# Moving a rounding step from ScalarE to GpSimd, and 256 columns of a sum from VectorE to ScalarE, in a four-layer convolution kernel

## Chip, cores and metric

The kernel runs on one core of a Trainium2 chip, as one launch. The metric is device time in microseconds: the median over several executions of the same program. All times below are in microseconds unless they are marked ns. Engine names: PE is TensorE, DVE is VectorE, ACT is ScalarE, POOL is GpSimd, SP is SyncE, which here only issues DMAs.

## What is computed

The state `x` has shape 32x32x32x32 (batch, then three axes that each layer reads in its own way). Four layers follow one another, and each adds its result to the state:

```
x = x + L0(gn(x))   # locally connected 3x3, signs of the weights, batch norm, relu, sign * mean
x = x + L1(gn(x))   # locally connected 3x3, plain f32 weights
x = x + L2(gn(x))   # like L0, other weights
x = x + L3(gn(x))   # products of all pairs of a row's elements, then a matmul
```

`gn` is a group normalisation. In L0 and L2 the weights (9.4 million numbers, used once each) enter as `sign(w) * mean(|w|)`, so the kernel needs both the sign of every weight and the sum of the absolute values of all of them:

```
def binarize(x):
    scale = jnp.mean(jnp.abs(x))
    return jnp.sign(x) * scale
...
wb = binarize(weight)[0]
out = jnp.einsum('bchwk,ochwk->bohw', patches, wb)
```

## The kernel before

**Tiling.** The image has 8 blocks (`BLOCKS`) of four rows by 4 pieces (`PIECES`) of eight columns, so each of the first three layers is 32 chunks, numbered n = 4m + j. A chunk of weights is one DMA of 128 x 2304 f32 numbers (1152 KB) into a ring of 8 slots, `wring`. A piece of the state is 128 x 256 numbers. Pieces are normalised in an order of their own, numbered e: `order(m, j)` takes blocks 0 and 1 alternately for the first `FRONT` = 8 pieces and is 4m + j after that. A chunk needs its own piece and the pieces above and below it. `needed(n)` is the last of these, e = n + 4 for n from 4 to 27.

**What a chunk of the first and third layers takes.**

- SP issues the load of chunk n once both `signs_made` and `abs_made` say that chunk n - 8 has been read (line 284), since its slot is then free.
- DVE sums the absolute values of the first `ABS_DVE` = 2048 columns (line 738). After chunks with n % 4 = 3 and n % 4 = 0 it evacuates one half row of results from PSUM: a transpose (line 730) and a sum (line 732). It waits for the convolution there.
- ACT sums the absolute values of the other 256 columns (line 509, an `ACTIVATE` with a read of the accumulator behind it) and writes the signs of all 2304 columns in f16 (line 510). After n % 4 = 1 and 2 it squares a half row of results, 512 columns, also with an accumulator (line 537).
- The normalised pieces are f32 and are split in two f16 halves: the high half is the f32 value rounded to f16, the low half is the rest. For e < 8 DVE normalises, for e >= 8 POOL does, with a subtraction and a multiplication (line 265). In both cases **ACT makes the high half** (line 517, `high_half`) and **POOL the low half** (line 372, `low_half`), which reads the high half.
- POOL copies the chunk's own piece, both halves, to `near` (line 383). ACT's queue issues two DMAs of 32 KB which bring the rows above and below to `beyond` (line 526), once the piece `needed(n)` has been normalised.
- PE waits for `near`, `beyond` and the signs, then runs the chunk's matmuls (line 890).

**The order of each queue is written out by hand.** Iteration n of ACT is: high halves up to e = needed(n) + 2, the wait that conv n - 4 is done, the wait for piece needed(n) and the two `beyond` DMAs, the wait for sign n - 1, absolute sum n, sign n, and in some iterations the square. Iteration n of POOL is: for each new e up to needed(n) + 2 the two normalising instructions and the low half of piece e - 1; then `near` n. In both, iteration 3 takes e = 8 and 9, iteration 4 takes e = 10, and from there on each takes one, up to e = 31 in iteration 25. Iterations 26 to 31 normalise nothing. Absolute sums and signs 0 and 1 are put ahead of the loop, while the group normalisation's statistics are still being made.

`xn_ring` holds 4 normalised pieces in f32, and a piece may be written when the low half of the piece 4 before it has been made. An instruction of POOL that reads what the POOL instruction before it wrote waits on a semaphore for it, as ACT and DVE do too.

Of the kernel before, what the change touches and what calls it, by code (L numbers as in the profile page):

```python
# [23 lines left out]
CHUNKS = BLOCKS * PIECES  # L24
# [1 line left out]
REACH = TAPS * C  # L26
CHUNK = KINDS * COLS * REACH
PIECE = COLS * B
ABS_DVE = 2048
SLOTS = 8  # L30
FIRST_SLOT = (0, 0, 4)
FRONT = 8
PE_SUMS = (((0, 3), (3, 6)), ((0, 4), (4, 8)))
DVE_SQUARES = 5
XSLOTS = 4
# [38 lines left out]
def build(nc, x, w_conv, bias, gamma_beta, w_pairs, mats, sel_rows, sel_index, out):  # L74
    ctx = ExitStack()
    with ctx:
        def sb(name, shape, dt):
            return ctx.enter_context(nc.sbuf_tensor(name, shape, dt))

        def sem(name):  # L80
            return ctx.enter_context(nc.semaphore(name))

        def sems(name, n):
            return [sem(f"{name}{i}") for i in range(n)]
# [8 lines left out]
        xn_ring = sb("xn_ring", [P, XSLOTS, PIECE], F32)  # L93
# [17 lines left out]
        row_id = sb("row_id", [P, 1], F32)  # L111
        unused = sb("unused", [P, CHUNK - ABS_DVE], BF16)

# [39 lines left out]
        centred = sem("centred")  # L153
        xn_made = sem("xn_made")
        hi_made = sem("hi_made")
        front_made = sem("front_made")
        norm_made = sems("norm_made", 3)
        squares = sems("squares", 4)
# [52 lines left out]
        def blk(t, m):  # L211
            return t[:, m * BLOCK:(m + 1) * BLOCK]
# [4 lines left out]
        def normed(layer, m, j):  # L217
            aux = states[layer][1]
            first = (m + 1) * BLOCK + j * PIECE
            return aux[:, first:first + PIECE]  # L220

        def at(e):

            return (e % 2, e // 2) if e < FRONT else divmod(e, PIECES)
# [4 lines left out]
        def needed(n):  # L229

            m, j = divmod(n, PIECES)
            return order(min(m + 1, BLOCKS - 1), j)

        def slot(layer, n):
            return (n + FIRST_SLOT[layer]) % (PIECES if layer == 1 else SLOTS)
# [31 lines left out]
        def halves(layer, e):  # L267
            m, j = at(e)
            return normed(layer, m, j).bitcast(F16).rearrange("p (k n) -> p k n", k=2)
# [82 lines left out]
        def _(pool):  # L352
# [6 lines left out]
            def xn_of(layer, e, made):  # L359

                if layer != 1:
                    pool.wait_ge(norm_made[layer], e - XSLOTS + 1)
                sub, mul = normalise(pool, layer, e)
                sub().then_inc(centred, 1)
                centre[0] += 1
                pool.wait_ge(centred, centre[0])
                mul().then_inc(made, 1)

            def low_half(layer, e):
                pool.wait_ge(hi_made, CHUNKS * (layer // 2) + e + 1)  # L370
                hv = halves(layer, e)
                pool.tensor_tensor(hv[:, 1, :], xn_ring[:, e % XSLOTS, :], hv[:, 0, :], ALU.subtract).then_inc(norm_made[layer], 1)

# [13 lines left out]
            def sum_squares(layer, m):  # L387

                pool.wait_ge(squares[layer], m + 1)
                sq = blk(states[layer][1], m)  # L390
                width = BLOCK // 2
                while width > B:
                    pool.tensor_tensor(sq[:, 0:width], sq[:, 0:width], sq[:, width:2 * width], ALU.add).then_inc(halved, 1)  # L393
                    halvings[0] += 1
                    pool.wait_ge(halved, halvings[0])
                    width //= 2
                pool.tensor_tensor(red[:, 1, m * B:(m + 1) * B], sq[:, 0:B], sq[:, B:2 * B], ALU.add).then_inc(gn_red_pool[layer], 1)

            for layer in range(3):
                if layer < 2:  # L400
                    for m in range(DVE_SQUARES, BLOCKS):
                        sum_squares(layer, m)
                pool.wait_ge(gn_ready[layer], 1)
                ready = 0
                for n in range(CHUNKS):
                    upto = min(CHUNKS, needed(n) + 3)
                    for e in range(ready, upto):
                        if e >= FRONT:
                            xn_of(layer, e, norm_made[1] if layer == 1 else xn_made)
                        if layer != 1 and e:  # L410
                            low_half(layer, e - 1)
                        if layer != 1 and e == CHUNKS - 1:
                            low_half(layer, e)
                    ready = max(ready, upto)
                    copy_near(layer, n)
# [73 lines left out]
        def _(act):  # L489
# [13 lines left out]
            def sign_of(layer, n):  # L503
# [3 lines left out]
                if done:  # L507
                    act.wait_ge(signs_made, done)
                act.activation(unused[:, :], wring[:, slot(layer, n), ABS_DVE:], ACT.Abs, accum_out=abs_sums[:, CHUNKS + n:CHUNKS + n + 1])
                act.activation(signs[:, n % PIECES, :], wring[:, slot(layer, n), :], ACT.Sign).then_inc(signs_made, 1)  # L510

            def high_half(layer, e):
                if e < FRONT:
                    act.wait_ge(front_made, FRONT * layer + e + 1)
                else:
                    act.wait_ge(xn_made, (CHUNKS - FRONT) * (layer // 2) + e - FRONT + 1)
                act.activation(halves(layer, e)[:, 0, :], xn_ring[:, e % XSLOTS, :], ACT.Copy).then_inc(hi_made, 1)

            def load_beyond(layer, n):
# [28 lines left out]
            for layer in range(3):  # L548
                scratch = states[layer][1]
                if layer < 2:  # L550
                    square(layer)
                if layer == 0:
                    act.wait_ge(sums_cleared, 1)
                    act.wait_ge(sel_made, 1)
                if layer == 2:
                    act.wait_ge(conv_done, CHUNKS * 2)
                    act.wait_ge(row_summed, 2 * BLOCKS)
                if layer != 1:
                    for n in range(2):
                        sign_of(layer, n)  # L560
                width = MB if layer < 2 else 512
                take_root(rstd[:, 0:width], tmp_a[:, 0:width], (1, 3, 4)[layer])
                if layer == 1:
                    for n in range(CHUNKS):
                        m, j = divmod(n, PIECES)
                        used(1, n)
                        load_beyond(1, n)
                        act.activation(rest[:, j, :].rearrange("p (q h b) -> p q h b", q=2, b=B),  # L568
                                       state_a[:, 0:STATE].rearrange("p (q h b) -> p q h b", q=BLOCKS, b=B)
                                       [:, 2 * j:2 * j + 2, PIECES * m:PIECES * (m + 1), :], ACT.Copy).then_inc(rest_made, 1)  # L570
                        if n > PIECES and j in (1, 2):
                            square_row(2 * (m - 1) + j - 1)
                    for e in range(2 * BLOCKS - 2, 2 * BLOCKS):
                        square_row(e)
                    continue
                m2 = layer // 2
                ready = 0
                for n in range(CHUNKS):
                    upto = min(CHUNKS, needed(n) + 3)
                    for e in range(ready, upto):  # L580
                        high_half(layer, e)
                    ready = max(ready, upto)
                    used(layer, n)
                    load_beyond(layer, n)
                    if n >= 2:
                        sign_of(layer, n)
                    if n > PIECES and n % PIECES in (1, 2):
                        square_half(layer, 2 * (n // PIECES - 1) + n % PIECES - 1)
                for e in range(2 * BLOCKS - 2, 2 * BLOCKS):
                    square_half(layer, e)  # L590
                take_root(sc[:, 11:12], sc[:, 15:16], (2, 0, 5)[layer])

                for m in range(BLOCKS):
                    act.wait_ge(bn_affine[m2], m + 1)
                    act.activation(blk(scratch, m), blk(scratch, m), ACT.Relu,
                                   accum_out=relu_sums[:, m:m + 1]).then_inc(relu_made[m2], 1)
                for m in range(MASKS, BLOCKS):
                    act.wait_ge(relu_made[m2], m + 1)
                    act.activation(blk(scratch, m), blk(scratch, m), ACT.Sign).then_inc(masks_made[m2], 1)
# [43 lines left out]
        def _(dve):  # L643
# [30 lines left out]
            for layer in range(3):  # L674
# [59 lines left out]
                for n in range(CHUNKS):  # L734
                    dve.wait_ge(w_in[slot(layer, n)], 16 * loads(layer, n))
                    if n == 0 and m2:
                        dve.wait_ge(abs_red[0], 1)
                    dve.tensor_reduce(abs_sums[:, n:n + 1], wring[:, slot(layer, n), 0:ABS_DVE],  # L738
                                      X, ALU.add, apply_absolute_value=True).then_inc(abs_made, 1)
# [361 lines left out]
```

## Time and profile before

| | |
|---|---|
| median of 3 runs | 745.15 us (741.66 to 745.32) |
| the profiled execution | 743.5 us, of which the span from first to last instruction is 741.7 us |
| mean granted TensorE clock | 0.876 of full speed |
| busy share of the span | PE 69%, DVE 75%, ACT 59%, POOL 57% |
| first layer's chunk loop | about 45 to 140 us of the span |
| second layer's | about 190 to 312 us |
| third layer's | about 339 to 434 us |
| fourth layer | the rest |

The busy shares are averages over four layers whose limits differ; what the change is worth must be read from the chunk loops of the first and the third layer alone. A row of a timeline gives the start, the length, the engine, the line, the operation, output <- inputs and, in brackets, how long the engine had been idle and what released it. ACTq and SPq are the queues on which ACT and SP issue DMAs, so a row of ACTq is an issue and not a transfer. Lengths overlap the next instruction a little, so what an instruction costs its engine is the distance from its start to the next one's.

### The profile page before, as it was taken

The page shows a single profiled execution, that of the slowest core. Times are in us where ns is not written, and L with a number is a line of the kernel's source. Part 1 is how long each engine was busy: PE and PEld are TensorE (multiplying, and loading weights), DVE is VectorE, ACT ScalarE, POOL GpSimd, SP SyncE. Part 2 cuts the span into 40 slices and gives each one's busy share as a digit, 9 for nine tenths or more (in the row PEclk, how much of TensorE's full clock was granted, in tenths as well). Part 3 has the DMA queues.
Part 4 walks back from the last instruction along what each step waited for, and adds up shares of the span by engine and source line. Part 5 has one row for each costly group of instructions (what it writes and reads, how often), then busy time and mean ns, then how long its engine had stood idle before and what let it go on. Part 6 is the DMA issues. An engine that isn't in the chain of part 4 may idle for free.

```text
span 741.7 us, 53863 instructions
## 1 busy us (share of the span) xinstructions
PE 508.3 (69%) x24648; PEld 394.2 (53%) x24648; DVE 558.1 (75%) x691; ACT 436.2 (59%) x741; POOL 421.9 (57%) x653
## 2 busy tenths in 40 slices
PE   4548655418699999715756523726898898987997
PEld 4537655317578888604646521203565565554665
DVE  4798999898634323379999989954588787786887
ACT  5459999492112212136999938323567766675665
POOL 3389884004545541019888200546779878878662
PEclk9856899759799999975898975967899999999999
DMA  8949999400289999915999930015799999999995
GB/s 335 423 162 395 390 397 396 183 0 1 92 319 355 381 397 398 415 53 196 396 396 400 378 134 1 0 28 160 266 305 393 383 331 400 363 335 371 325 396 224
DMA packets 38882, 209.09 MB, mean 282 GB/s; under 512 B 7216, under 2 KB 14384, under 8 KB 18352
## 3 DMA queue, kind: packets, MB, share of 16 engines
q1 hardware_dynamic: 29376, 201.67, 71.5%
q10 hardware_dynamic: 9216, 6.30, 2.8%
q0 software_dynamic: 240, 0.53, 0.2%
q8 instruction: 22, 0.36, 0.2%
q14 instruction: 28, 0.23, 0.1%
HBM read 193.79 MB, written 4.19 MB: 267 GB/s over the span
## 4 chain that ended last, share of the span: by engine, by line
PE 34%; DVE 18%; DMA 17%; POOL 10%; issue 10%; ACT 8%; ACTq 2%; SPq 0%; POOLq 0%; DVEq 0%
PE psum L890 13%; DMA wring<-in_pairs 6%; PE psum L1003 6%; PE psum L977 5%; PE psum L914 5%; ACT signs L510 4%; DMA beyond<-state_a 3%; POOL xn_ring L265 3%; DMA wring<-in_w 3%; DMA beyond<-state_b 3%; DVE xn_ring L265 2%; PE psum L900 2%; DVE state_a L798 2%; ACTq L526 2%; ACT state_b L638 2%
## 5 line engine op out<-in xcount | busy, mean ns | idle before, releaser
L853 DVE TENSOR_TENSOR state_b<-psum,state_b 128x512 f32<-128x512 f32 x256 | 167.5, 686 | 56.9 <-ACT state_b L638 52.9
L890 PE MATMUL psum<-signs,near 64*32 64x96 f16 (+3 forms) x6528 | 125.0, 217 | 100.8 <-DMA beyond<-nothing 39.3
L638 ACT ACTIVATE state_b<-psum 128x512 f32<-128x512 f32 x256 | 142.0, 595 | 85.3 <-PE psum L977 79.4
L890 PEld LDWEIGHTS psum<-signs,near 64*32 64x32 f16 (+1 forms) x6528 | 112.3, 103 | 109.6 <-issue 109.2
L738 DVE TENSOR_REDUCE abs_sums<-wring 128x1 f32<-128x2048 f32 x64 | 142.9, 2276 | 0.1
L510 ACT ACTIVATE signs<-wring 128x2304 f16<-128x2304 f32 x64 | 135.0, 2109 | 0.0
L1003 PE MATMUL psum<-state_b,wring 128*32 128x32 f32 x8192 | 106.1, 202 | 10.9 <-issue 6.0
L1003 PEld LDWEIGHTS psum<-state_b,wring 128*32 128x32 f32 x8192 | 88.4, 114 | 42.0 <-issue 21.9
L977 PE MATMUL psum<-signs,sel 64*128 64x512 f16 x516 | 89.3, 400 | 25.3 <-POOL signs L428 13.9
L890 PE MATMUL psum<-wring,near 64*32 64x96 f32 (+5 forms) x3264 | 96.1, 240 | 15.3 <-DMA beyond<-nothing 10.7
L428 POOL COPY signs<-wring 64x512 f16<-64x512 f16 x130 | 85.8, 660 | 34.2 <-PE psum L977 27.7
L890 PEld LDWEIGHTS psum<-wring,near 64*32 64x32 f32 (+1 forms) x3264 | 86.6, 108 | 22.2 <-issue 22.2
L383 POOL COPY near<-state_b 128x512 f16<-128x512 f16 (+1 forms) x64 | 33.2, 521 | 72.5 <-PE psum L900 53.4
L709 DVE STREAM_TRANSPOSE state_b<-psum 128x512 f32<-128x512 f32 x16 | 11.5, 717 | 75.2 <-PE psum L900 75.2
L890 PE MATMUL psum<-signs,beyond 32*32 32x96 f16 (+2 forms) x2176 | 64.3, 215 | 0.0
L890 PEld LDWEIGHTS psum<-signs,beyond 32*32 32x32 f16 x2176 | 55.0, 101 | 4.7
L447 POOL COPY wring<-state_b 32x256 f32<-32x256 f32 x128 | 50.4, 394 | 10.1
L890 PE MATMUL psum<-wring,beyond 32*32 32x96 f32 (+2 forms) x1088 | 49.4, 239 | 1.3 <-issue 1.3
L977 PEld LDWEIGHTS psum<-signs,sel 64*128 64x128 f16 x516 | 23.6, 94 | 46.7 <-ACT state_b L638 24.8
L568 ACT ACTIVATE signs<-state_a 128x256 f32<-128x256 f32 x32 | 13.3, 417 | 59.2 <-issue 49.3
L393 POOL TENSOR_TENSOR state_b<-state_b 128x512 f32<-128x512 f32 (+3 forms) x24 | 16.7, 696 | 53.6 <-ACT state_b L501 52.2
L890 PEld LDWEIGHTS psum<-wring,beyond 32*32 32x32 f32 x1088 | 43.3, 106 | 5.2 <-issue 2.0
(151 smaller groups left out, 873.9 us busy)
## 6 DMA issues: line engine op xcount, KB each, us to landing
wring<-in_w SPq DMA_DIRECT2D x96, 1152.0 KB, 10.0
wring<-in_pairs SPq DMA_DIRECT2D x64, 1152.0 KB, 9.1
state_a<-in_x SPq DMA_DIRECT2D x8, 512.0 KB, 9.5
beyond<-state_b ACTq DMA_DIRECT2D x112, 32.0 KB, 5.9
wring<-signs SPq DMA_DIRECT2D x56, 64.0 KB, 4.9
out<-state_a SPq DMA_DIRECT2D x7, 512.0 KB, 11.3
beyond<-state_a ACTq DMA_DIRECT2D x56, 32.0 KB, 6.0
beyond<-nothing ACTq DMA_DIRECT2D x24, 32.0 KB, 4.2
```

Of the source, the lines that this page charges most:

```text
L265: return (lambda: eng.tensor_tensor(new, old, m_op, ALU.subtract)), (lambda: eng.tensor_tensor(new, new, r_op, ALU.mult))
L383: pool.tensor_copy(dst, src).then_inc(near_made, 1)
L428: pool.tensor_copy(ring[side * 2 * W:(side + 1) * 2 * W, k % GROUP, :].rearrange("p (g n) -> p g n", g=G), parts[0:2 * W, k // KPART % 2, ...
L447: pool.tensor_copy(own_x[beside * W:(beside + 1) * W, g % 2, cols], x_sq[g * W:(g + 1) * W, half, :]).then_inc(own_copied, 1)
L510: act.activation(signs[:, n % PIECES, :], wring[:, slot(layer, n), :], ACT.Sign).then_inc(signs_made, 1)
L638: act.activation(left[:, n % LSLOTS, :], psum[:, n % ASLOTS, :], ACT.Copy, scale=1.0 / HALF_SCALE / HALF_SCALE).then_inc(left_made, 1)
L738: dve.tensor_reduce(abs_sums[:, n:n + 1], wring[:, slot(layer, n), 0:ABS_DVE], X, ALU.add, apply_absolute_value=True).then_inc(abs_made, 1)
L853: dve.tensor_tensor(feats[:, n % FSLOTS, :], psum[:, ASLOTS + n % BSLOTS, :], left[:, n % LSLOTS, :], ALU.mult).then_inc(feats_made, 1)
L890: last = pe.matmul(psum[g * B:(g + 1) * B, bank, (a * C) % 512:(a * C) % 512 + (b - a) * C], acts[q, j, s, k, :], weights[q, j, kind, s, ( ...
L914: pe.matmul(psum[:, 4, first * B:end * B], same_half, by_h[:, h, first:end, :], start=(first == 0 and h == 0), stop=(h == H - 1), skip_gro ...
L977: last = pe.matmul(psum[:, bank, :], sel[half, t % PT * P:(t % PT + 1) * P], ring[half, t // PT, :], start=True, stop=True)
L1003: last = pe.matmul(psum[g * W:(g + 1) * W, 6 + s // HALF, col:col + B], wt[:, t % PT, c, g, :], f[:, g, c, :], start=False, stop=(t % (HAL ...
```

## The change

For e >= 8, in the first and third layers, the high half is made by POOL with a copy from f32 to f16 instead of by ACT. POOL then makes both halves of piece e right after normalising it, and waits for its own multiplication ahead of the high half and for its own high half ahead of the low half. The low halves of pieces 0 to 7 stay on POOL and their high halves on ACT, in the order in which they were (the low half of piece e - 1 behind the normalisation of e). `ABS_DVE` goes from 2048 to 1792: in every chunk of these two layers DVE sums 256 columns fewer and ACT 512 instead of 256. The scratch tile `unused` grows with it. Nothing else is changed.

```
-ABS_DVE = 2048
+ABS_DVE = 1792
...
+            def high_half(layer, e):                        # POOL
+                pool.wait_ge(xn_made, (CHUNKS - FRONT) * (layer // 2) + e - FRONT + 1)
+                pool.tensor_copy(halves(layer, e)[:, 0, :], xn_ring[:, e % XSLOTS, :]).then_inc(hi_pool, 1)
+                pool.wait_ge(hi_pool, (CHUNKS - FRONT) * (layer // 2) + e - FRONT + 1)
+
             def low_half(layer, e):
-                pool.wait_ge(hi_made, CHUNKS * (layer // 2) + e + 1)
+                if e < FRONT:
+                    pool.wait_ge(hi_made, FRONT * (layer // 2) + e + 1)
...
                         if e >= FRONT:
                             xn_of(layer, e, norm_made[1] if layer == 1 else xn_made)
-                        if layer != 1 and e:
+                        if layer != 1 and 0 < e <= FRONT:
                             low_half(layer, e - 1)
-                        if layer != 1 and e == CHUNKS - 1:
+                        if layer != 1 and e >= FRONT:
+                            high_half(layer, e)
                             low_half(layer, e)
...
             def high_half(layer, e):                        # ACT
-                if e < FRONT:
-                    act.wait_ge(front_made, FRONT * layer + e + 1)
-                else:
-                    act.wait_ge(xn_made, (CHUNKS - FRONT) * (layer // 2) + e - FRONT + 1)
+                act.wait_ge(front_made, FRONT * layer + e + 1)
...
                     upto = min(CHUNKS, needed(n) + 3)
-                    for e in range(ready, upto):
+                    for e in range(ready, min(upto, FRONT)):
                         high_half(layer, e)
```

## Rows read from the trace of the kernel before

**Rows 1.** Window, first layer: length, busy PE, PEld, DVE, ACT, POOL, clock, DMA share, GB/s
```profile
70.00:80.00 10.00, 5.49 (x465) 5.02 (x469) 9.96 (x7) 10.00 (x18) 8.48 (x13) 1.00 1.03 393
```

**Rows 2.** Timeline of ACT, one chunk of the first layer, next one's start
```profile
74.26 0.41 ACT L517 ACTIVATE state_b<-xn_ring 128x256 f16<-128x256 f32 x1
74.57 0.41 ACT L509 ACTIVATE unused<-wring 128x256 bf16<-128x256 f32 x1
...
74.97 2.11 ACT L510 ACTIVATE signs<-wring 128x2304 f16<-128x2304 f32 x1
76.98 0.41 ACT L517 ACTIVATE state_b<-xn_ring 128x256 f16<-128x256 f32 x1
```

**Rows 3.** Chain that ended last, first layer's end: start, length, what
```profile
131.35 6.31 DMA beyond<-state_b
...
137.75 1.63 PE psum L890 x128
```

**Rows 4.** Timeline of POOL, first layer, one iteration without idle time
```profile
52.86 0.73 POOL L265 TENSOR_TENSOR xn_ring<-state_a,stats 128x256 f32<-128x256 f32 x1
53.66 0.72 POOL L265 TENSOR_TENSOR xn_ring<-xn_ring,stats 128x256 f32<-128x256 f32 x1
54.35 0.67 POOL L372 TENSOR_TENSOR state_b<-xn_ring,state_b 128x256 f16<-128x256 f32 x1
54.96 0.60 POOL L383 COPY near<-state_b 128x512 f16<-128x512 f16 x1
55.53 0.72 POOL L265 TENSOR_TENSOR xn_ring<-state_a,stats 128x256 f32<-128x256 f32 x1
```

**Rows 5.** Line 383 in the second layer: duration ns min/median/max, span of starts
```profile
L383 POOL COPY near<-state_b x31: 396/396/590, 190.7 to 297.3; 128x256 f32<-128x256 f32 x31
```

**Rows 6.** Timeline of POOL, first layer: piece 8, and the last low half
```profile
45.40 0.72 POOL L265 TENSOR_TENSOR xn_ring<-state_a,stats 128x256 f32<-128x256 f32 x1
...
46.88 0.67 POOL L372 TENSOR_TENSOR state_b<-xn_ring,state_b 128x256 f16<-128x256 f32 x1
...
116.49 0.67 POOL L372 TENSOR_TENSOR state_b<-xn_ring,state_b 128x256 f16<-128x256 f32 x1 [2.05 <-ACT state_b L517]
```

**Rows 7.** Timeline of ACT and its queue, first layer: chunks 3, 27 and 30
```profile
50.34 0.42 ACT L509 ACTIVATE unused<-wring 128x256 bf16<-128x256 f32 x1 [0.85 <-POOL state_b L372]
...
119.53 0.51 ACTq L526 DMA_DIRECT2D beyond<-state_b  x1
...
122.36 0.41 ACT L509 ACTIVATE unused<-wring 128x256 bf16<-128x256 f32 x1
...
130.62 0.40 ACT L509 ACTIVATE unused<-wring 128x256 bf16<-128x256 f32 x1
```

**Rows 8.** ACT's squares of 512 columns, first layer: ns min/median/max
```profile
L537 ACT ACTIVATE stats<-state_b x16: 612/619/632, 58.2 to 140.2; 128x512 f32<-128x512 f32 x16
```

**Rows 9.** Loads of weights in two stretches: issue ns, starts, time to landing
```profile
L276 SPq DMA_DIRECT2D wring<-in_w x4: 327/328/328, 109.6 to 117.5; - x4
DMA to landing us min/median/max: 12.0/13.3/13.9
L276 SPq DMA_DIRECT2D wring<-in_w x3: 328/328/328, 121.1 to 125.5; - x3
DMA to landing us min/median/max: 13.3/14.2/14.7
```

**Rows 10.** Third layer: piece 8 on POOL, sign 27 on ACT
```profile
339.33 0.72 POOL L265 TENSOR_TENSOR xn_ring<-state_b,stats 128x256 f32<-128x256 f32 x1
...
416.72 2.11 ACT L510 ACTIVATE signs<-wring 128x2304 f16<-128x2304 f32 x1
```

**Rows 11.** DVE's reductions by shape, whole run: busy us, mean ns of one
```profile
L738 DVE TENSOR_REDUCE abs_sums<-wring 128x1 f32<-128x2048 f32 x64 | 142.9, 2276 | 0.1
L722 DVE TENSOR_REDUCE sc<-bias 128x1 f32<-128x256 f32 x2 | 0.8, 420 | 0.1
```

**Rows 12.** Page, DMA issues: count, KB each, median us to landing
```profile
beyond<-nothing ACTq DMA_DIRECT2D x24, 32.0 KB, 4.2
```

More of the change, by code:

```diff
@@ L155, in build @@
         hi_made = sem("hi_made")
+        hi_pool = sem("hi_pool")
         front_made = sem("front_made")
```

## The prediction

> **What bounds the kernel now.** I read the page first, for the shares of busy time, and set them aside: they average four layers. The windows of the chunk loop [rows 1] come next. There ACT is busy for all of the 10 us, DVE for 9.96, the DMA engines the whole time, POOL for 8.48. So ACT and DVE share the pace, the loads are close behind, and POOL has 1.5 us in 10 to spare. The timelines say what each needs for a chunk. An ACT chunk [rows 2] is 0.31 for the high half (74.26 to 74.57), 0.40 for the absolute sum and its read, 2.01 for the sign: 2.72 us. Two chunks in four have a square as well, with its read some 0.61, so 3.33; the mean is 3.02. POOL, when it waits for nobody [rows 4], takes 0.80 + 0.69 + 0.61 + 0.57 = 2.67 us for an iteration. It is quicker than ACT by a third of a microsecond, and waits for ACT's high half to fall back to its pace.
>
> The chain of waits tells what ends a layer [rows 3]: the last chunk's matmuls (1.63 us, from 137.75) begin when the `beyond` DMA issued at 131.35 has landed, 6.31 us later. That DMA stands in ACT's queue right behind absolute sum 30, at 130.62 [rows 7]. After the matmuls come one evacuation and the batch norm, which the change does not touch. So what counts is by how much this issue moves, once in the first and once in the third layer.
>
> **The change, part by part.**
>
> DVE: 256 columns fewer. From 2048 and 256 columns [rows 11], a column costs (2276 - 420) / 1792 = 1.036 ns, so 265 ns a chunk, 8.5 us of DVE's time a layer. Its cover is complete: after it DVE needs less than ACT in every chunk, and DVE issues nothing on which the last `beyond` waits. What it can give is an earlier release of slots, and loads don't want it: the load of chunk 31 is among those issued from 109.6 to 117.5, which land within 13.9 us [rows 9], while ACT reads chunk 31 only some 3 us after 130.62. Price 0, unless ACT's part makes DVE matter.
>
> ACT: 256 columns more, 24 high halves fewer. 512 columns with a read cost 619 ns [rows 8] against 405 for 256 [rows 2], +0.21 in each chunk. A high half is 0.31. So a chunk up to 25 gets 0.10 cheaper (2.62, or 3.23 with a square), those from 26 on 0.21 dearer. Absolute sums 0 and 1 lie ahead of the loop, where ACT waits for the statistics anyway: 0.
>
> POOL: 24 high halves a layer, and two waits for its own results in each. It shows no f32 to f16 copy. The nearest row is the copy of 256 columns from f32 to f32, 0.396 us at the median [rows 5]. The copy of 512 f16 columns takes 0.60 [rows 4] and is the upper bound. The low half, too, writes f16 and takes 0.67 against 0.73 for its like with f32 results [rows 4], so narrowing is no extra cost, and I take 0.396. The lower bound is 0.396 less the 0.1 by which neighbours overlap when no wait stands between them, about 0.30. A wait for its own result costs 0.08: the multiplication starts 0.80 after a subtraction of 0.73. Before, the low half that follows the multiplication was of another piece and started 0.69 after it; now it is the copy, at 0.81. The new iteration is 0.81 + 0.81 + 0.48 + 0.61 + 0.57 = 3.28 us, 0.61 more than 2.67. **That is above ACT's new 2.62 and 3.23, so POOL sets the pace.**
>
> The Trainium skill, "GPSIMD Engine Reference", Engine selection, says that one-input operations on GpSimd run at roughly line rate and warns only of two-input ones. By its 1.2 GHz 256 columns are an estimated 0.21 us, and the 0.21 between the copies of 256 and 512 columns in [rows 4, 5] agrees; the rest of the 0.396 is a fixed cost, which that rule leaves out. With 0.21 for the whole copy the iteration would be 3.09 and the loss below would fall by 4 us a layer.
>
> When does POOL end? It starts piece 8 at 45.40 [rows 6]. Piece 8 now takes 0.81 + 0.67 (to 46.88, as before), low half 7 0.63, high half 0.48, low half 0.63, so piece 9 starts at 48.64; that one takes 0.81 + 0.81 + 0.48 + 0.61 and `near` 0.57, and piece 10 starts at 51.92. Then 21 iterations of 3.28 us bring piece 31 to 120.80, and its low half ends 0.81 + 0.81 + 0.48 + 0.67 later, at **123.57**. Before, it ended at 117.16 [rows 6].
>
> Who waits for it? ACT's queue, in iteration 27: the two `beyond` DMAs of chunk 27 need piece 31, and behind them in the queue stand absolute sum and sign 27. Before, they were issued from 119.53, with no wait [rows 7]. Two issues are 1.16 us and the dispatch some 0.07, so absolute sum 27 starts at 124.80 instead of 122.36: **+2.44**. (It is a steady state: by the same rule ACT starts sum n at least 1.23 us after low half n + 4, and as 3.28 is more than either of ACT's periods, it is caught near chunk 10.) From there nothing waits for POOL but 3 longer absolute sums (27, 28, 29) lie before the last issue, +0.63. So the last `beyond` leaves 3.07 us later, at 134.42. It lands 6.31 later as before: the loads have the same bytes and the last of them (issued at 125.5, 14.7 to landing, [rows 9]) lands at 140.2 in the old trace, so the DMA engines are still full when it leaves. Chunk 31's matmuls end 3.07 later; PE has idle time in front of each chunk and its own work is unchanged. In the third layer sign 27 comes 77.39 after piece 8's subtraction [rows 10], in the first 77.36 (sum 27's 122.36 + 0.40 - 45.40), so the lag is the same.
>
> **Sum:** 2 x 3.07 = +6.1 us. Against the profiled execution's own time: 743.5 + 6.1 = 749.6. The median of the runs is 745.15, 1.65 above that execution, and 745.15 + 6.1 = 751.3. I give 750.5, between the two.
>
> **Rivals.**
>
> *ACT keeps the pace (the other side).* Chunk 3 no longer stands behind high halves 8 and 9: its `beyond` waits for low half 7 (47.53 in the sum above), two issues 1.16, so its absolute sum starts at 48.7 instead of 50.34 [rows 7], -1.6. Iterations 4 to 25 lose 22 high halves (-6.8), chunks 3 to 29 gain 27 x 0.21 (+5.7): together -2.7 a layer, -5.4 in all, 738 to 740 us. For it speak ACT's full windows and POOL's spare time [rows 1]. It decides if low half 31 is there by 117.8, an iteration of 3.01 us: high half and both waits would have to cost 0.34, not 0.61. An iteration of 3.14 gives no change. The Trainium skill ("Perfetto Trace Analysis", Identifying the Most-Contended Engine) says to optimise the busiest engine first. By that rule this is the outcome, since ACT and DVE are busier than POOL here; the rows of POOL's iteration are against it.
>
> *The copy costs as much as one of 512 columns.* 0.60 for 0.396 is 22 x 0.20 = +4.5 a layer: 759 to 760 us. For it: no row shows this conversion. Against it: the f16 results of the low half are not slow.
>
> *POOL's lag is absorbed by the transfers.* In the new pace, 3.28 a chunk, the loads fall less far behind, and the last `beyond` might land in 4.2 us, as those from `nothing` do at the median [rows 12], instead of 6.31. Then the loss is 1.0 a layer, +1.9 in all, 746 to 747. Against it: 140.2 above.
>
> *The waits are partly cheaper than I count* (the copy at its lower bound, 0.30): -2.1 a layer, +1.9 in all, the same time.
>
> **How the numbers follow.** Runs of this kernel differ by 0.5% (741.66 to 745.32), which is what a measurement can tell. Chances: POOL sets the pace at about the price worked out 0.55; dear copy 0.13; transfers absorb it or cheaper waits 0.20; ACT keeps the pace 0.12. Slower by over 0.5% (+3.7 us) are the first two: 0.68. Same 0.20. Faster 0.12. The range holds the first three cases, from 744 (the third, with the spread of the runs) to 758, which leaves out part of the dearest copies. The likeliest case's own range is 747 to 755.
>
> **What the profile would show.** POOL's copy of 128x256 f16 from f32 at 0.40, a POOL iteration of 3.28 without idle time from piece 10 on, and the last low half ending near 123.6 and 418. ACT idle some 0.05 to 0.65 a chunk from chunk 10 or so, released by POOL's low half (line of `low_half`), absolute sums at 0.62, DVE's at 2.01 with idle time in front of its transposes. The last `beyond` issue near 134.4, the first layer's matmuls ending at 142.5, the third's 3 later relative to its start. If POOL's iteration is under 3.14 us, or the last `beyond` takes 4 us, the prediction is wrong.

## The result and the profile after

The changed kernel takes 748.92 us (median of 8 runs, 746.6 to 754.23) against 743.64 us for the kernel before (8 runs, 741.66 to 747.85). The medians differ by 5.3 us. The ratio estimated from all runs is 1.0088, that is 6.5 us slower, with a 95% interval of 1.0055 to 1.012 (4.1 to 8.9 us). The forecast was +6.1 us and a time of 750.5 (744 to 758). Ratios below are all to runs of the kernel before that were made beside the experiment.

The page of the changed kernel has a span of 749.5 us. DVE's busy time fell from 558.1 to 542.1 us, POOL's rose from 421.9 to 442.3, ACT's stayed (436.2, 438.1). Over the whole run no engine's busy share moved by more than three points, so the shares don't show where the loss comes from.

POOL, timeline of the first layer, one iteration and the last low half, to be laid beside [rows 4, 6]:

```profile
51.66 0.73 POOL L266 TENSOR_TENSOR xn_ring<-state_a,stats 128x256 f32<-128x256 f32 x1
52.47 0.72 POOL L266 TENSOR_TENSOR xn_ring<-xn_ring,stats 128x256 f32<-128x256 f32 x1
53.25 0.40 POOL L372 CAST state_b<-xn_ring 128x256 f16<-128x256 f32 x1
53.73 0.67 POOL L379 TENSOR_TENSOR state_b<-xn_ring,state_b 128x256 f16<-128x256 f32 x1
54.34 0.61 POOL L390 COPY near<-state_b 128x512 f16<-128x512 f16 x1
54.91 0.73 POOL L266 TENSOR_TENSOR xn_ring<-state_a,stats 128x256 f32<-128x256 f32 x1
...
122.32 0.67 POOL L379 TENSOR_TENSOR state_b<-xn_ring,state_b 128x256 f16<-128x256 f32 x1
```

An iteration is 3.25 us here, 3.27 in the mean of the 21 from piece 10 to piece 31; the only gaps are the 0.06 to 0.08 behind an instruction whose result the next one waits for. The last low half ends at 122.99, 5.83 after the old one. The new line, `high_half`, by source: ns min/median/max, first and last start:

```profile
L372 POOL CAST state_b<-xn_ring x24: 392/397/398, 47.3 to 121.8; 128x256 f16<-128x256 f32 x24
L372 POOL CAST state_a<-xn_ring x24: 397/398/399, 347.2 to 421.7; 128x256 f16<-128x256 f32 x24
```

ACT and its queue, timeline of the first layer: chunks 26, 27 and 30, beside [rows 7]:

```profile
119.82 1.16 ACTq L531 DMA_DIRECT2D beyond<-state_b  x2
121.08 0.63 ACT L517 ACTIVATE unused<-wring 128x512 bf16<-128x512 f32 x1
...
123.08 1.16 ACTq L531 DMA_DIRECT2D beyond<-state_b  x2
124.34 0.63 ACT L517 ACTIVATE unused<-wring 128x512 bf16<-128x512 f32 x1
...
133.25 0.61 ACT L517 ACTIVATE unused<-wring 128x512 bf16<-128x512 f32 x1
133.98 0.62 ACTq L531 DMA_DIRECT2D beyond<-state_b  x1
```

The queue issues the two `beyond` DMAs of chunk 27 at 123.08, 0.09 after piece 31's low half ended at 122.99, and sum 27 starts 1.26 later. That is the handover by which POOL's lag reaches ACT. It is so at every chunk from 10 to 27 (in the third layer from 9): the first of the two issues comes 0.09 after the low half that it needs, where in the kernel before it came 2.0 us or more after it. Chunk 10, POOL's low half of piece 14 and the issue behind it:

```profile
66.80 0.67 POOL L379 TENSOR_TENSOR state_b<-xn_ring,state_b 128x256 f16<-128x256 f32 x1
...
67.55 0.51 ACTq L531 DMA_DIRECT2D beyond<-state_b  x1
```

The view of waits does not name this handover: in the first layer's loop it gives ACT only 3.2 us of idle time, released by its own sign, because it sees the engine and not the queue that stands in front of it. The two times side by side show it.

Window of the changed kernel, in the columns of [rows 1]: POOL is the one without spare time at 9.33 (the gaps behind its waits for its own results, 0.22 in an iteration of 3.27, make up the rest), ACT and DVE are not full any more.

```profile
100.00:110.00 10.00, 6.18 (x432) 5.59 (x420) 7.41 (x8) 8.66 (x12) 9.33 (x17) 0.84 1.02 395
```

Chain that ended last, at the ends of the first and the third layer, beside [rows 3]:

```profile
133.98 5.79 DMA beyond<-state_b
...
139.86 1.63 PE psum L895 x128
...
434.09 6.84 DMA beyond<-state_a
...
441.30 2.15 PE psum L895 x128
```

The last matmuls of the third layer take 2.15 us and not 1.63 (as in the first layer, and in both layers before) because TensorE's granted clock fell while they ran: it was 1.00 of full speed from 436 to 441 us, when PE was busy for 2.0 of the 5 us, 0.98 from 441.2 to 442.2, and half, 1.2 GHz, after that:

```profile
442.20:443.40 1.20, 1.20 (x64) 1.06 (x56) 0.00 (x0) 0.00 (x0) 0.00 (x0) 0.50 0.00 0
```

The clock is lower elsewhere in the loops too (0.78 from 95 to 140 us, 0.92 before). It is not what delays the `beyond` DMAs up to chunk 27, which leave 0.09 after POOL's low halves; what it adds to the lateness of single matmuls I did not separate.

To compare kernels I take four points of each loop, counted from the start of piece 8's subtraction on POOL: the end of the last low half; the start of DVE's evacuation 13 (the transpose of the half row whose square stands in ACT's queue ahead of the last `beyond`); the last `beyond` issue; and the start of the last transpose (which follows the last matmuls). First layer / third layer, from the timelines:

| kernel | last low half | evacuation 13 | last `beyond` issue | last transpose | ratio of times |
|---|---|---|---|---|---|
| before | 71.8 / 71.8 | 83.45 / 83.64 | 85.95 / 85.97 | 94.0 / 94.6 | 1 |
| changed | 77.8 / 77.8 | 87.27 / 87.56 | 88.79 / 89.01 | 96.3 / 98.4 | 1.0088 |
| sums_only | 76.8 / 76.5 | 88.15 / 88.17 | 92.11 / 91.72 | 99.3 / 100.8 | 1.0149 |
| halves_only | 77.8 / 77.8 | 87.63 / 87.69 | 89.08 / 89.13 | 96.9 / 98.9 | 1.0102 |
| copy_twice | 89.0 / 89.0 | 97.89 / 97.92 | 100.12 / 99.94 | 107.3 / 108.6 | 1.0373 |
| near_cut | 69.8 / 69.8 | 82.97 / 82.46 | 86.68 / 85.89 | 94.9 / 94.6 | 1.0019 |
| near_cut_before | 73.4 / 71.8 | 85.25 / 83.56 | 87.64 / 85.96 | 95.8 / 94.5 | 1.0019 |
| two_scratch | 71.8 / 71.8 | 83.82 / 84.46 | 85.58 / 85.91 | 93.6 / 95.0 | 1.0016 |
| near_cut_two_scratch | 69.8 / 69.8 | 80.72 / 79.61 | 83.89 / 83.08 | 91.9 / 91.8 | 0.9961 |
| two_scratch_after | 77.8 / 77.8 | 87.68 / 87.37 | 89.13 / 88.82 | 97.2 / 98.3 | 1.0099 |
| split | 70.0 / 69.9 | 84.84 / 84.41 | 86.29 / 85.86 | 94.2 / 94.9 | 1.0024 |
| split_1920 | 71.4 / 70.4 | 84.73 / 84.68 | 87.13 / 86.16 | 96.3 / 95.2 | 1.0036 |
| near_dve | 66.5 / 66.6 | 85.41 / 83.71 | 86.86 / 85.16 | 94.9 / 93.7 | 0.9974 |

The column of evacuation 13 shows a second way into the last issue, which the prediction left out: in `halves_only`, `split`, `near_dve` and `two_scratch_after` the last `beyond` leaves 1.45 us after evacuation 13 starts, in both layers. There DVE holds it, through the square. In the changed kernel the distance is 1.52 and 1.45, so ACT and DVE arrive nearly together; in the kernel before it is 2.50 and 2.33, and DVE is out of the way.

The two loops account for 2.3 + 3.8 = 6.1 us of the 7.8 between the two profiled executions. The other 1.7 are stretches that the change does not touch (second layer +1.7, from its end to piece 8 +1.7, from the third layer's last transpose on -1.8, and smaller ones); the ratio over all runs, at 6.5 us, does not have them at that size.

### The profile page after: what moved, and what is told of

Read it like the earlier page. It is cut to its first block, busy times and chain, and to the rows that moved or that the text cites. A ratio compares the mean times of both kernels' runs of the same rounds, so it can differ in the third digit from the quotient of the medians.

```text
span 749.5 us, 53863 instructions
## 1 busy us (share of the span) xinstructions
PE 518.5 (69%) x24648; PEld 402.6 (54%) x24648; DVE 542.1 (72%) x691; ACT 438.1 (58%) x693; POOL 442.3 (59%) x701
## 4 chain that ended last, share of the span: by engine, by line
PE 34%; DVE 18%; DMA 17%; POOL 14%; issue 7%; ACT 7%; ACTq 2%; SPq 1%; DVEq 0%; POOLq 0%
PE psum L895 13%; DMA wring<-in_pairs 7%; PE psum L1008 6%; POOL xn_ring L266 5%; PE psum L982 5%; DMA wring<-in_w 5%; PE psum L919 5%; DMA beyond<-state_b 3%; ACT signs L518 3%; POOL near L390 2%; DVE xn_ring L266 2%; ACTq L531 2%; DVE state_a L803 2%; PE psum L994 2%; DVE state_b L858 2%
## 5 line engine op out<-in xcount | busy, mean ns | idle before, releaser
L895 PE MATMUL psum<-signs,near 64*32 64x96 f16 (+3 forms) x6528 | 134.8, 225 | 97.1 <-DMA beyond<-nothing 32.9
L895 PEld LDWEIGHTS psum<-signs,near 64*32 64x32 f16 (+1 forms) x6528 | 120.9, 108 | 106.7 <-issue 106.4
L743 DVE TENSOR_REDUCE abs_sums<-wring 128x1 f32<-128x1792 f32 x64 | 125.8, 2009 | 0.1
L1008 PE MATMUL psum<-state_b,wring 128*32 128x32 f32 x8192 | 105.0, 201 | 10.9 <-issue 5.9
L895 PE MATMUL psum<-signs,beyond 32*32 32x96 f16 (+2 forms) x2176 | 69.1, 223 | 0.0
L895 PEld LDWEIGHTS psum<-signs,beyond 32*32 32x32 f16 x2176 | 59.3, 106 | 5.2
L517 ACT ACTIVATE unused<-wring 128x512 bf16<-128x512 f32 x64 | 40.1, 626 | 13.8 <-ACT signs L518 6.2
## 6 DMA issues: line engine op xcount, KB each, us to landing
wring<-in_w SPq DMA_DIRECT2D x96, 1152.0 KB, 11.2
```

What stands on the lines that cost most here:

```text
L895: last = pe.matmul(psum[g * B:(g + 1) * B, bank, (a * C) % 512:(a * C) % 512 + (b - a) * C], acts[q, j, s, k, :], weights[q, j, kind, s, ( ...
L1008: last = pe.matmul(psum[g * W:(g + 1) * W, 6 + s // HALF, col:col + B], wt[:, t % PT, c, g, :], f[:, g, c, :], start=False, stop=(t % (HAL ...
```

## The experiments

### The two halves of the change, each alone

`sums_only`, on the kernel before, nothing else:

```
-ABS_DVE = 2048
+ABS_DVE = 1792
```

> The kernel before with the absolute sums moved alone (DVE 1792 columns, ACT 512); all high halves stay on ACT. Theory (ACT and POOL pace the loops, DVE's saving is hidden): ACT's chunk is 0.21 us longer with its high half in it, 2.93 and 3.54 us, mean 3.24 for 3.02, so the last beyond issue of a layer comes some 5.5 us later and the kernel takes +11 us, about 755 against 744. POOL waits for ACT's high half more than before. Rival (DVE set the pace together with ACT): DVE's 8.5 us a layer come back in part, the time is 744 or less.

Measured: 752.67 us, ratio 1.0149 (1.0108 to 1.019). ACT's last `beyond` issue comes 6.2 and 5.8 us later, where 5.5 were expected. POOL waits for ACT's high half, as this row of its timeline shows:

```profile
121.71 0.67 POOL L372 TENSOR_TENSOR state_b<-xn_ring,state_b 128x256 f16<-128x256 f32 x1 [2.27 <-ACT state_b L517]
```

So DVE's 8.5 us a layer are worth nothing where ACT sets the pace, and ACT's 0.21 a chunk is worth its full sum (+11.1 us by the ratio, +11 expected).

`halves_only`, on the changed kernel:

```
-ABS_DVE = 1792
+ABS_DVE = 2048
```

> The changed kernel with the absolute sums put back (DVE 2048 columns, ACT 256): the high halves alone are moved. Theory: POOL's iteration stays at 3.27 us and its last low half at 123.0 us, ACT waits for it up to chunk 27 as in the changed kernel, and only the three shorter sums 27 to 29 differ (-0.63 us a layer): about +2.3 us a layer, +4.6 us, ratio about 1.006. Rival (the longer absolute sums caused the loss): the kernel is as quick as before or quicker, ratio 1.000 or less, since ACT has lost 24 instructions a layer.

Measured: 749.94 us, ratio 1.0102 (1.0064 to 1.014). The last low half comes at 77.8, as in the changed kernel, so POOL's part is as expected and the rival has fallen. But the last issue is 3.1 us late in the first layer and 3.2 in the third, not 2.3. DVE's timeline of the first layer, with the last issue below it:

```profile
129.90 0.72 DVE L735 STREAM_TRANSPOSE state_b<-psum 128x512 f32<-128x512 f32 x1 [1.56 <-PE psum L895]
...
133.45 0.71 DVE L735 STREAM_TRANSPOSE state_b<-psum 128x512 f32<-128x512 f32 x1
...
134.80 6.66 DVE L743 TENSOR_REDUCE abs_sums<-wring 128x1 f32<-128x2048 f32 x3
141.37 0.70 DVE L735 STREAM_TRANSPOSE state_b<-psum 128x512 f32<-128x512 f32 x1
...
142.72 0.71 DVE L735 STREAM_TRANSPOSE state_b<-psum 128x512 f32<-128x512 f32 x1
```

```profile
134.90 0.61 ACTq L531 DMA_DIRECT2D beyond<-state_b  x1
```

The late matmuls make DVE wait (1.56 at 129.90). With 2048 columns it can't make that up: evacuation 13 starts at 133.45, ACT's queue holds the square of it ahead of the last `beyond`, and that leaves at 134.90. At the end of the first layer DVE's own work is last: three sums of 6.66 us together and two transposes without idle time in between. (In the third layer DVE waits 1.83 for the last matmuls.) In the changed kernel evacuation 13 starts at 132.45, and at the end of both layers DVE waits for matmuls. So the smaller sums on DVE take back about what the longer sums on ACT cost: the two kernels' intervals overlap almost wholly, though ACT's last three sums in `halves_only` are 0.6 shorter in all.

### POOL's length, doubled and cut

`copy_twice`:

```
+                for k in range(2):
+                    pool.tensor_copy(halves(layer, e)[:, 0, :], xn_ring[:, e % XSLOTS, :]).then_inc(hi_pool, 1)
+                    pool.wait_ge(hi_pool, 2 * ((CHUNKS - FRONT) * (layer // 2) + e - FRONT) + k + 1)
```

> The changed kernel with POOL's high half made twice, each copy followed by the wait for it. Theory: POOL's iteration goes from 3.27 to 3.27 + 0.48 = 3.75 us, the last low half comes 24 x 0.48 = 11.5 us later in each of the two layers, and all of it arrives at the end: +23 us over the changed kernel, +29 us over the kernel before, ratio about 1.039. Rival (slack downstream takes up POOL's lag, and the loss has another cause): clearly less than half of that.

Measured: 769.78 us, ratio 1.0373 (1.033 to 1.0415), 21 us over the changed kernel by the ratios. POOL's pair of casts and the last low half:

```profile
54.75 0.86 POOL L373 CAST state_b<-xn_ring 128x256 f16<-128x256 f32 x2
...
134.02 0.67 POOL L380 TENSOR_TENSOR state_b<-xn_ring,state_b 128x256 f16<-128x256 f32 x1
```

Against the changed kernel the last low half is 11.2 us later in each layer, the last issue 11.3 and 10.9, the last transpose 10.9 and 10.2. What POOL is given arrives at the end, almost undiminished.

`near_cut`, the opposite (most of the copy to `near` is left out):

```
+                if layer != 1 and n >= PIECES:
+                    dst, src = dst[:, 0:64], src[:, 0:64]
                 pool.tensor_copy(dst, src).then_inc(near_made, 1)
```

> The changed kernel with POOL's copy to near cut to 64 of 512 columns from chunk 4 on (first and third layers), so this part of the computation is left out; all instructions and waits stay. Theory: POOL's iteration falls by about 0.35 us to 2.92 us, less than ACT's mean chunk, so ACT sets the pace. ACT's chunk without a high half takes 2.82 us (no square) and 3.24 us (square) in the changed kernel's trace, mean 3.03 against 3.02 before, so the time comes back to about the kernel before, ratio 0.998 to 1.002. Rival (the prediction's case of ACT keeping the pace with chunks of 2.62 and 3.23 us): -5.4 us against the kernel before, ratio 0.993. Rival (POOL's length does not matter): as the changed kernel, 1.009.

Measured: 744.01 us, ratio 1.0019 (0.9992 to 1.0046). The copy is shorter by 0.38, and the iteration is 2.89 in the mean:

```profile
54.23 0.23 POOL L392 COPY near<-state_b 128x64 f16<-128x64 f16 x1
54.43 0.73 POOL L266 TENSOR_TENSOR xn_ring<-state_a,stats 128x256 f32<-128x256 f32 x1
```

The loss is gone and the kernel is where the old one was. The prediction's own rival, ACT at a pace of 2.62 and 3.23 us with -5.4 us, is not what happens once POOL is out of the way.

`near_cut_before` is the control: the same cut on the kernel before.

> Control: the kernel before with the same cut of POOL's copy to near (64 of 512 columns from chunk 4 on, the rest left out). Theory: POOL's iteration is 0.37 us shorter, but here it waits for ACT's high half anyway, so its idle time grows and nothing else: ratio 0.997 to 1.003, last beyond issue at its old place, 86 us after piece 8's subtraction. Rival (the copy loads something that the other engines share, and near_cut was quick for that reason): clearly quicker than before, by some 5 us.

Measured: 743.88 us, ratio 1.0019 (0.9984 to 1.0054); the last issue in the third layer at 85.96 (before 85.97), in the first at 87.64, 1.7 late in the profiled execution, for a cause that stays open. The cut by itself gives nothing, so `near_cut` was quick because POOL's iteration had been what the changed kernel waited for.

### Why ACT gained nothing

Without a high half in between, ACT's absolute sum n stands right behind sign n - 1 and waits for it. A chunk without a square in `near_cut`, timeline of ACT:

```profile
64.26 0.63 ACT L519 ACTIVATE unused<-wring 128x512 bf16<-128x512 f32 x1
...
64.89 2.11 ACT L520 ACTIVATE signs<-wring 128x2304 f16<-128x2304 f32 x1
67.09 0.63 ACT L519 ACTIVATE unused<-wring 128x512 bf16<-128x512 f32 x1
```

From sign to sum are 2.20 us, where in [rows 2] the next instruction, a high half that waits for no sign, started after 2.01. The chunk is 2.83 instead of 2.62, more than the old 2.72. The wait is there because all sums write to the one scratch tile `unused`. To take it away, I gave the sums two scratch tiles in turn:

```
-                if done:
-                    act.wait_ge(signs_made, done)
-                act.activation(unused[:, :], ...
+                if done > 1:
+                    act.wait_ge(signs_made, done - 1)
+                act.activation(unused[:, done % 2, :], ...
```

On the kernel before, as `two_scratch`:

> The kernel before with two scratch tiles for ACT's absolute sums in turn, so that sum n waits for sign n - 2 instead of n - 1 and ACT's queue gets to the next beyond DMAs a chunk earlier. Theory (the last beyond issue ends the layer): it then waits only for the square that stands ahead of it, which waits for DVE's evacuation 13, ended at 129.6 instead of sum 30 dispatched at 130.7: -1.1 us a layer, -2.2 us, ratio 0.997. Rival (ACT's throughput alone ends the layer): chunks 28 to 31 lose 0.2 us each where no square stands between, ratio 0.999 to 1.000.

Measured: 743.89 us, ratio 1.0016 (0.9981 to 1.0051). The last issue is at 85.58 and 85.91, -0.4 and -0.1 of the 1.1 expected. The time shows no gain. The theory took evacuation 13 to stay where it was; it started 0.4 and 0.8 later, and in the third layer the last issue follows it by the 1.45 us of the table, so there DVE held it.

On `near_cut`, as `near_cut_two_scratch`:

> near_cut (POOL's copy to near cut to 64 columns, the rest left out) with the two scratch tiles for ACT's absolute sums. Theory (an ACT chunk without a square takes 2.82 us, not 2.62, since with the high half gone nothing covers the wait for sign n - 1): the wait for sign n - 2 is over long before, so these chunks fall to 2.62 us and ACT's mean to 2.93. With some 13 such chunks a layer ahead of the last beyond issue that is -2.6 us a layer, -5 us in all against near_cut, ratio about 0.995 against the kernel before. Rival (the 0.2 us has another cause): as near_cut, 1.002.

Measured: 739.77 us, ratio 0.9961 (0.9932 to 0.999). The same chunk as above:

```profile
63.81 0.61 ACT L519 ACTIVATE unused<-wring 128x512 bf16<-128x512 f32 x1
...
64.42 2.11 ACT L520 ACTIVATE signs<-wring 128x2304 f16<-128x2304 f32 x1
66.44 0.61 ACT L519 ACTIVATE unused<-wring 128x512 bf16<-128x512 f32 x1
```

2.63 us, as the prediction had taken it. Against `near_cut` the time fell by 4.3 us by the ratios, of the 5 expected.

On the changed kernel, as `two_scratch_after`:

> The changed kernel with the two scratch tiles alone. Theory (POOL sets the pace up to chunk 27): ACT's shorter chunks are given back as waits for POOL's low half; the beyond DMAs of chunk 27 leave as before, and only sums 28 and 29 gain 0.2 us each: -0.4 us a layer at most, ratio 1.007 to 1.009. Rival (ACT's own length decides): -2.6 us a layer, ratio about 1.002.

Measured: 749.44 us, ratio 1.0099 (1.0068 to 1.013). With POOL at 3.27 a quicker ACT gives nothing; even the -0.4 a layer from sums 28 and 29 is missing (the last issue is at 89.13 and 88.82, 88.79 and 89.01 in the changed kernel), since evacuation 13 holds it in both layers.

### Versions meant to be quicker

`split` (POOL makes the high halves of the pieces with e % 4 = 0 or 3 only):

```
+        def by_pool(e):
+            return e >= FRONT and e % 4 in (3, 0)
```

> The kernel before, with POOL making the high halves of only 12 of the 24 pieces (e % 4 = 0 and 3, those that ACT would make in its iterations with a square) and ACT the others; sums stay 2048 and 256. Theory (each engine's own work for four chunks decides): POOL 2 x 3.27 + 2 x 2.67, mean 2.97 us, ACT mean 2.87, both below the old 3.02, DVE unchanged at 2.87. So POOL's lag does not arise, and the last beyond issue moves until DVE's evacuation 13 holds it, about -1.1 us a layer: ratio 0.996 to 0.998. Rival (any high half on POOL delays the end in proportion): half of the loss of the changed kernel or of halves_only, ratio about 1.005.

Measured: 743.12 us, ratio 1.0024 (0.9991 to 1.0057). POOL's lag is gone (last low half at 70.0), so the rival has fallen, but the expected 2 us did not come. DVE's timeline in the first layer, its only wait up to then and the end:

```profile
62.44 0.72 DVE L747 STREAM_TRANSPOSE state_b<-psum 128x512 f32<-128x512 f32 x1 [3.15 <-PE psum L907]
...
131.21 0.71 DVE L747 STREAM_TRANSPOSE state_b<-psum 128x512 f32<-128x512 f32 x1
...
132.55 6.66 DVE L755 TENSOR_REDUCE abs_sums<-wring 128x1 f32<-128x2048 f32 x3
139.13 0.70 DVE L747 STREAM_TRANSPOSE state_b<-psum 128x512 f32<-128x512 f32 x1
```

DVE waits for matmuls early, 3.15 us at 62.44 (2.73 in the third layer), and with 2048 columns it works without idle time from there on and does not catch up. Evacuation 13 starts 1.4 and 0.8 us later than in the kernel before, and the last issue follows it by 1.45 in both layers. So relieving ACT alone hands the last issue to DVE. Why DVE's early wait is longer than the 1.76 and 1.44 of the kernel before was not tested.

`split_1920` (with the two scratch tiles and `ABS_DVE = 1920`):

> split with the two scratch tiles and 1920 columns on DVE, 384 on ACT. Theory: DVE gets 0.13 us a chunk cheaper (2.73) so that it no longer holds the last squares, ACT 0.11 dearer (mean 2.98, less 0.2 in the last chunks without a square), POOL 2.97: the last beyond issue comes some 1 to 2 us earlier a layer than in the kernel before, ratio 0.995 to 0.997. Rival (ACT's length decides alone): ratio 0.999 to 1.001.

Measured: 745.0 us, ratio 1.0036 (1.0007 to 1.0065). It is not quicker, and by its interval slightly slower; last issue at 87.13 and 86.16. I did not find out which of its three edits costs what.

`near_dve` (the changed kernel with two scratch tiles, and with DVE making the copies to `near` from chunk 4 on; POOL's `copy_near` returns at once there):

```
+                def copy_near(n):
+                    mm, j = divmod(n, PIECES)
+                    wait_normed(dve, layer, order(mm, j))
+                    dve.wait_ge(conv_done, CHUNKS * layer + n - PIECES + 1)
+                    dve.wait_ge(near_made, CHUNKS * layer + n)
+                    dve.tensor_copy(near[:, j, :].bitcast(F16), normed(layer, mm, j).bitcast(F16)).then_inc(near_made, 1)
...
+                    if PIECES <= n + 1 < CHUNKS:
+                        copy_near(n + 1)
                     dve.wait_ge(w_in[slot(layer, n)], 16 * loads(layer, n))
```

> A version meant to win: the changed kernel (high halves of e >= 8 on POOL, DVE 1792 columns) with the two scratch tiles, and with POOL's copies to near 4 to 31 of the first and third layers made by DVE, each ahead of the absolute sum of the chunk before. Nothing is left out. Theory: POOL's iteration loses 0.57 us (3.27 to 2.70), ACT's mean chunk is 2.93, DVE's is 2.60 plus a copy of 512 f16 columns, which no trace here shows on DVE; if it is 0.3 us DVE stands at 2.9. Then no engine needs more than the old 3.02 and the time is that of near_cut_two_scratch, ratio about 0.996. Rival (DVE becomes late, since its copies stand behind its waits for evacuations, or its copies and POOL's two-input instructions hold one another up as at 36 to 44 us): POOL's iteration is longer than 2.8 us or matmuls wait for near, ratio 1.00 or more.

Measured: 742.3 us against 744.6, ratio 0.9974 (0.994 to 1.0008). Three of DVE's copies:

```profile
63.71 0.28 DVE L748 COPY near<-state_b 128x512 f16<-128x512 f16 x1
...
65.84 0.78 DVE L748 COPY near<-state_b 128x512 f16<-128x512 f16 x1
...
114.23 0.28 DVE L748 COPY near<-state_b 128x512 f16<-128x512 f16 x1
```

The copy takes 0.28 us in some places and up to 0.85 in others, and POOL's iteration is 2.73 in the mean of the 21 from piece 10 on. The kernel is quicker than the changed kernel by 1.1% by the ratios; against the kernel before its interval still includes no difference, so it is not shown to be quicker. Its last issue follows evacuation 13 by 1.45 in both layers, so DVE, now with the copies, holds the end.

## Why the prediction was right, and where it was off

**POOL sets the pace at 3.28 us: right.** 3.27 measured. The conversion, which no row of before showed, costs 0.397, the value taken from the f32 copy (0.396). The wait for its own result costs 0.08, as taken. The last low half was forecast 78.2 after piece 8's subtraction and came 77.8 after it.

**The lag reaches ACT's queue at chunk 27 and from there the last `beyond`: right.** +3.07 a layer forecast, +2.84 and +3.04 measured. `copy_twice` and `near_cut` with its control show that this is the cause and not only a coincidence of numbers. In the parts of the sum, absolute sum 27 came 2.2 later in both layers, forecast 2.44: POOL's lag was 0.4 less, the handover 0.1 to 0.2 more (1.35 and 1.42 from low half to sum, forecast 1.23). From there to the last issue it was +0.65 in the first layer, by the three longer sums as forecast, but +0.80 in the third, where DVE's evacuation 13 held it. The sum had no term for that.

**ACT is caught near chunk 10: right for its queue, wrong for its sums, without effect on the total.** The queue issues right behind POOL's low half from chunk 10 on. But the sums start right behind the issues only from chunk 17 on (16 in the third layer; sum 17 starts at 91.68 after 0.23 idle), since ACT loses less a chunk against POOL than forecast. The mis-sized term is ACT's chunk without a square, 2.62 forecast and 2.83 measured. The prediction took the high half's 0.31 out and left the rest as it was, but the high half had covered 0.1 of the wait for the sign before, and 0.1 of overlap with its neighbour went as well. The trace of the kernel before held the clue, in the chunks without a high half behind 122.36 of [rows 7]:

```profile
124.97 0.42 ACT L509 ACTIVATE unused<-wring 128x256 bf16<-128x256 f32 x1
...
127.58 0.42 ACT L509 ACTIVATE unused<-wring 128x256 bf16<-128x256 f32 x1
```

They are 2.61 apart, where the prediction's terms (0.40 and 2.01) give 2.41.

**ACT keeps the pace, -5.4 us: this rival's price was wrong for the same reason.** With POOL shortened the kernel came back to 1.0019, not 0.993. Only with the wait removed too did part of it appear (0.9961). So with POOL out of the way the change as it stands still gained nothing that could be measured: in a chunk without a square, moving the high half off ACT gave back 0.1, since a wait came out from under it, and the added columns took 0.21.

**DVE's saving has price 0 since its cover is complete: true where ACT sets the pace (`sums_only`), not for the whole change.** The prediction said that DVE issues nothing on which the last `beyond` waits. It does: evacuation 13, through the square ahead of that DMA in ACT's queue. POOL's lag delays the matmuls, DVE waits for them and afterwards has more to make up. `halves_only` has the last issue 0.1 to 0.3 later than the changed kernel although its last three sums are 0.63 shorter, so the 1792 columns gave back some 0.8 a layer there.

**The transfer lands 6.31 us later as before: right in the mean.** 5.79 in the first and 6.84 in the third layer (before 6.31 and 6.60), and the last matmuls of the third took 2.15 instead of 1.63, at the lower clock. These made +2.3 and +3.8 out of +2.8 and +3.0. That the two loops add up to just the forecast 6.1 us is therefore part luck: -0.5 in one layer and +0.8 in the other, neither forecast, nearly cancel. The rival with a landing after 4.2 us has fallen.

**The dear copy: fallen**, by 0.397. So is the case of cheaper waits: an iteration of 3.27 leaves it no room. The time itself came out 1.6 us under the 750.5 given: 0.8 since the kernel before has a median of 743.64 over its eight runs, where the forecast counted from 744.4, and 0.8 since the medians differ by 5.3 and not by 6.1.

## What to carry to other kernels

When work moves to the engine with the most idle time, compare its length for one iteration of the loop, waits for its own results included, with the pace of the loop, and not its busy share: 85% busy and a ring of instructions that is 0.35 us shorter than the pace can't take 0.6 us more. An instruction taken off a busy engine is worth its length only if nothing was hidden behind it; look at the distance between the same two instructions in a stretch that never had it. Where two engines are tied, relief must reach both, and whoever stands between them in a queue (here the two `beyond` DMAs behind a wait) carries the delay on.

## What the runs showed of the hardware

- POOL: a cast of 128x256 from f32 to f16 takes 0.397 us, no more than a copy in f32 (0.396); a copy of 128x64 f16 takes 0.23 and one of 128x512 f16 0.61, so a column costs 0.85 ns and some 0.18 us of each does not depend on the columns (an estimate from two points, which gives 0.39 for 256 columns).
- ACT: an absolute sum that waits for the sign in front of it starts 2.20 us after the sign's start, one that need not wait 2.02 after: 0.18 us for a wait on the same engine's last result, in a chunk of 2.6.
- DVE: a copy of 128x512 f16 takes 0.28 us in some places of `near_dve` and 0.62 to 0.85 in others. POOL's timeline beside the first two copies shown above:

```profile
60.98 0.73 POOL L266 TENSOR_TENSOR xn_ring<-xn_ring,stats 128x256 f32<-128x256 f32 x1
...
63.69 0.89 POOL L266 TENSOR_TENSOR xn_ring<-xn_ring,stats 128x256 f32<-128x256 f32 x1
...
65.74 0.73 POOL L266 TENSOR_TENSOR xn_ring<-state_a,stats 128x256 f32<-128x256 f32 x1
```

The short copy (63.71) starts with POOL's multiplication at 63.69, and that one takes 0.89 instead of 0.73. The long copy (65.84) starts 0.10 into POOL's subtraction, which keeps its 0.73 and ends at 66.47, and the copy ends 0.15 after it. One of the two is lengthened each time. The Trainium skill, "SBUF — State Buffer", section "Who interferes with whom", says that a DVE operation in a two-port mode and a GpSimd operation exclude one another. These rows agree with it, though none says in which mode the copy ran. So does the rest of the trace, which has stretches with POOL at work and without: of the 40 copies that start before POOL's last low half of their layer ends, 16 take 0.62 us or more; of the 16 that start behind it, when POOL does nothing, all take 280 to 285 ns. No run changes POOL's work alone to test it.
